# Another order of TensorE's work in each step of an attention: values of the preceding tile ahead of the second pair of scores, maxima behind it

## The chip, the cores and the metric

One core of a Trainium2 chip runs the whole program. The metric is the device time of one execution in microseconds, the median of several runs. One execution was also taken with the hardware profiler; its trace gives every row below.

## What is computed

The program is one block of a model on 8 batches of 256 channels and 1024 tokens: an attention with a position bias and a residual, a second attention with relative embeddings and a residual, and a routed feed-forward layer. The change is in the second attention only:

```
proj = jnp.einsum('bld,de->ble', x, W) + b            # x is (8, 1024, 256), normalised
q, k, v = jnp.split(proj.reshape(batch, length, 8, 96).transpose(0, 2, 1, 3), 3, axis=3)
qk = jnp.einsum('bhqd,bhkd->bhqk', q, k)
qe = jnp.einsum('bhqd,qkd->bhqk', q, embeddings)      # rotated sinusoids of q - k
weights = softmax((qk + qe) / sqrt(32), axis=-1)
output = jnp.einsum('bhqk,bhkd->bhqd', weights, v)
```

## The kernel before

The program runs its stages one after another: tables, the first token phase (projections), the first attention (names end in `_af`), the second token phase, the second attention (names end in `_kf`), and the feed-forward tail. Every engine has its own queue, worked off in the written order, and waits on semaphores.

The second attention works **keys first**: scores stand with keys on the partitions and queries along the free axis. A *unit* `u` is one batch, one group of four heads and 512 queries; there are 32 units. A unit has eight *steps*, one for each tile of 128 keys; step `n` counts through all units (256 steps), and `n % 8` is its place in the unit. In a step TensorE does, for the tile `n`:

- `scores(4n)`, the first pair: for heads 0 and 1 one product over 128 rows each (L1118), then one over 64 rows each (L1123) that adds the low halves and the row of maxima. The banks for scores are three, in a ring, so the score of head `s` waits until the exponential of `s - 3` has read its bank. `scores(4n + 2)` is the second pair, heads 2 and 3.
- `maxima(n)`: four products over 64 rows (L996) that form scores for the unit after next or the next one, only for their row maxima. VectorE reduces them (L1004, two in a step, in two banks used in turn). In step 6 a transpose of all row maxima of the next unit (L989) stands in front of them; VectorE copies it to `max_row` (L1006), and SyncE moves it with four small transfers (L981) into the row of `lows` that the next unit's scores read. The first scores of a unit wait for these transfers (semaphore `m_in`).
- `weigh(n - 1)`, the values of the preceding tile (L1143): four fp32 products of 32 columns each, side by side, added up over the unit in one bank, `out_ps`. They wait until all four exponentials of tile `n - 1` are there, and the first of a unit waits until the last unit's `out_ps` was copied (semaphore `taken`).
- `denominators`, the sums of the unit before, in step 1 (L1155): twelve fp32 products of the shape of L1143 over the last two tiles of exponentials and the sum of the other six, which GpSimd adds up (L1229). They go into one of the two banks of the maxima; VectorE copies them (L1248) and takes reciprocals in four pieces, one in each of steps 2 to 5 (L1242).

ScalarE takes the exponential of each head (L1199) into a ring of four tiles; for head 0 from the fifth tile on it also waits for the ring (`weighed`, and `acc_ok` or `max_full`). It copies the finished `out_ps` to `oS` (`take`, L1182) in the step that `TAKE` names, between heads 1 and 2. GpSimd multiplies and adds the residual behind its sums of step 5.

Of the kernel before, what the change touches and what calls it, by code (L numbers as in the profile page):

```python
# [10 lines left out]
def build(nc, x, gamma, wqkv, wout, w1q, b1cols, b1v, gatew, experts, relt, cw0, cb0, cw1, cb1, cw2, cb2,  # L11
# [30 lines left out]
    KTU = NT  # L42
# [14 lines left out]
    with ctx:  # L57
# [836 lines left out]
        def attention_keys_first():  # L894
            with ExitStack() as es:
# [31 lines left out]
                NU = NB * UB  # L927
# [43 lines left out]
                def queries(u):  # L971

                    return (u // NC) % G, (u % NC) * CH
# [10 lines left out]
                def max_product(pe, n, u, m, max_ps=max_ps):  # L984

                    slot, first = queries(u)
                    if m == MH:
                        pe.wait_ge(max_read, n)
                        nc.tensor.transpose(max_ps[n % len(max_ps)][0:HG * TT, 0:P], row_min[:], idf[:]).then_inc(max_full, 1)  # L989
                        return  # L990
                    if n >= len(max_ps):
                        pe.wait_ge(max_read, n + 1 - len(max_ps))
                    j, t = divmod(m, TT)
                    for c in range(NC):
                        half = slice(2 * D * c, 2 * D * (c + 1))
                        last = nc.tensor.matmul(max_ps[n % len(max_ps)][:, c * CH:(c + 1) * CH],  # L996
                                                stacks[half, slot, QHH, j, first + t * P:first + (t + 1) * P],
                                                stacks[half, slot, KHL, j, c * CH:(c + 1) * CH], start=True, stop=True)
                    last.then_inc(max_full, 1)
# [7 lines left out]
                                                ALU.mult).then_inc(max_read, 1)  # L1007

                AHEAD_ = KTU + 2
                DEN, REC, TAKE, FIN = 1, 2, 1, 5  # L1010
                first_jobs = [(0, m) for m in range(MJ)] + [(1, m) for m in range(2 * (AHEAD_ - KTU))]
                step_jobs = []
                for n in range(NU * KTU):
# [54 lines left out]
                with nc.Fori(0, B // NB) as i_:  # L1068
                    with nc.Block() as block:
# [37 lines left out]
                        @block.tensor  # L1107
                        def _(pe):
                            def scores(s):

                                u, (kt, j) = s // SU, divmod(s % SU, HG)
                                slot, first = queries(u)
                                if s % SU == 0 and u >= 1:
                                    pe.wait_ge(m_in[u % 2], 16 * HG * ((u + 1) // 2))
                                for i in range(2):
                                    if s + i >= 3:
                                        pe.wait_ge(exps, s + i - 2)
                                    nc.tensor.matmul(score_ps[(s + i) % 3], stacks[:, slot, KHL, j + i, kt * P:(kt + 1) * P],  # L1118
                                                     stacks[:, slot, QHH, j + i, first:first + CH], start=True, stop=False,
                                                     skip_group_check=True)  # L1120
                                for i in range(2):
                                    half = slice(2 * D * i, 2 * D * (i + 1))
                                    nc.tensor.matmul(score_ps[(s + i) % 3], lows[half, slot, KH1, j // 2, kt * P:(kt + 1) * P],  # L1123
                                                     lows[half, slot, QL, j // 2, first:first + CH], start=False, stop=True,
                                                     skip_group_check=True).then_inc(full, 1)

                            def maxima(n):
                                for u, m in step_jobs[n]:
                                    if m == 0 and u % NC == 0:
                                        q = u // NC  # L1130
                                        pe.wait_ge(stk[q % 2], LOADS * ((q + 1) // 2))
                                    max_product(pe, job_at[(u, m)], u, m)

                            def weigh(n):
                                u, kt = divmod(n, KTU)
                                g, bb = (u // NC) % G, u // UB
                                if kt == 0 and u % UB == 0 and bb >= 1:
                                    pe.wait_ge(v_in[bb % 2], 16 * ((bb + 1) // 2))
                                if kt == 0 and u >= 1:
                                    pe.wait_ge(taken, u)  # L1140
                                pe.wait_ge(exps, HG * (n + 1))
                                for j in range(HG):
                                    last = nc.tensor.matmul(out_ps[j * D:(j + 1) * D, :],  # L1143
                                                            V[:, bb % 2, kt, (g * HG + j) * D:(g * HG + j + 1) * D],
                                                            prob[:, n % PR, j, :], start=(kt == 0), stop=(kt == KTU - 1),
                                                            skip_group_check=True)
                                last.then_inc(weighed, 1)

                            def denominators(n, u):
                                pe.wait_ge(max_read, n - 1)  # L1150
                                pe.wait_ge(acc_ok, ADDS * (u + 1))
                                parts = [prob[:, (KTU * u + kt) % PR] for kt in range(ADDS + 1, KTU)] + [acc[:, u % 2]]
                                for i, part_ in enumerate(parts):
                                    for j in range(HG):
                                        last = nc.tensor.matmul(max_ps[n % 2][j * D:(j + 1) * D, 0:CH], den_w[:], part_[:, j, :],  # L1155
                                                                start=(i == 0), stop=(i == len(parts) - 1),
                                                                skip_group_check=True)
                                last.then_inc(max_full, 1)

                            for n in range(NU * KTU + DEN + 1):  # L1160
                                if n < NU * KTU:
                                    scores(HG * n)
                                summed = n >= KTU and n % KTU == DEN
                                if summed:
                                    denominators(job_at[(n // KTU - 1, "den")], n // KTU - 1)
                                elif n < NU * KTU:
                                    maxima(n)
                                if n < NU * KTU:
                                    scores(HG * n + 2)
                                    if summed:  # L1170
                                        maxima(n)
                                if 1 <= n <= NU * KTU:
                                    weigh(n - 1)

                        @block.scalar
                        def _(act):
# [26 lines left out]
                        def _(pool):  # L1203
                            def finish(u):

                                bb, g = u // UB, (u // NC) % G
                                _, first = queries(u)
                                pool.wait_ge(taken, u + 1)
                                pool.wait_ge(recd, PIECES * (u + 1))
                                if u >= 1:  # L1210
                                    pool.wait_ge(fin, u)
                                nc.gpsimd.tensor_tensor(oN[:], oS[:, u % 2, :], rec[:, u % 2, :], ALU.mult).then_inc(scaled, 1)
                                pool.wait_ge(x_in[bb % 2], 16 * (bb // 2 + 1))
                                pool.wait_ge(scaled, u + 1)
                                r = res_[:, bb % 2, g, first:first + CH]
                                nc.gpsimd.tensor_tensor(r, r, oN[:], ALU.add).then_inc(fin, 1)
# [266 lines left out]
        for kind, attention in enumerate((attention_first, attention_keys_first)):  # L1483
            stages = attention()
            early = next(stages)
            tables = setup(early) if kind == 0 else None
            token_phase(kind, early.rooms, early, tables)
            next(stages, None)
            if kind == 0:
                turned.close()  # L1490
# [493 lines left out]
```

## Time and profile before

| | before |
|---|---|
| median of 3 runs | 2847.14 us (2841.78 to 2848.37) |
| the profiled execution's own time | 2855.66 us |
| its span, first to last instruction | 2853.8 us |
| second attention, stretch 1509 to 2462 us of the span | 953 us |
| TensorE busy in it | 937.25 us |
| VectorE, ScalarE, GpSimd busy in it | 714.06, 571.87, 802.02 us |
| granted TensorE clock in it | 1.00 (2.4 GHz) |
| share of the 16 DMA engines in it | 0.24 |

A row of the timeline has the start in us from the span's start, the time from the first to the last instruction of the row, the engine (PE is TensorE's products, PEld its weight loads, DVE VectorE, ACT ScalarE, POOL GpSimd, SPq SyncE's queue), the line, what it writes and reads, the count, and in brackets how long the engine sat idle before it and what ended that. Products are pipelined: one of 512 columns is shown with some 0.39 us and the next one starts 0.21 us after it, so a wait between two products of one row shows as a longer row and not as idle time. What counts is from start to start.

### The profile page before, as it was taken

Reading aid. Unit: us, or ns where it says so; the run is one execution under the profiler, and the core shown is the slowest. Engines: PE = TensorE matmul, PEld = TensorE weight load, DVE = VectorE, ACT = ScalarE, POOL = GpSimd, SP = SyncE. Lnnn points to the kernel's source line nnn. Section 1 sums busy time; section 2 is a strip of 40 time slices with the busy share of each in tenths; the row PEclk is TensorE's granted clock in tenths of the full one; section 3 lists DMA queues with packets and bytes.
Section 4 is the critical chain, followed back from the end, with each engine's and each line's share of the span. In section 5 each row is a group of like instructions: output and inputs, shape, how many; then the busy total and the mean of one; then the engine's idle time right before and its main releaser. Section 6 shows DMA issues by size and latency. Waiting matters only on the chain. (4 is left out here: it accounts for less than half of the span.)

```text
span 2853.8 us, 47289 instructions
## 1 busy us (share of the span) xinstructions
PE 2481.0 (87%) x18516; PEld 817.5 (29%) x18516; DVE 1991.5 (70%) x3075; ACT 1402.8 (49%) x2548; POOL 1967.8 (69%) x763
## 2 busy tenths in 40 slices
PE   7899999999999999968988999999999999651255
PEld 2564222222222222235552222222222222240144
DVE  4475787787787787647886777877778777277134
ACT  3345555555555555523335565665656656440012
POOL 3114788888888888844446888888888888630763
PEclk9999999999999999989999999999999999775568
DMA  4994222322222322039764321223212230350337
GB/s 80 238 237 137 49 50 49 76 67 49 53 49 55 80 57 53 9 134 308 231 216 116 74 64 49 64 71 90 64 49 64 71 75 16 102 180 9 96 121 248
DMA packets 236267, 278.16 MB, mean 97 GB/s; under 512 B 65392, under 2 KB 171376, under 8 KB 232842
## 3 DMA queue, kind: packets, MB, share of 16 engines
q1 hardware_dynamic: 225548, 249.89, 32.3%
q0 software_dynamic: 6144, 16.85, 1.9%
q10 hardware_dynamic: 4352, 8.39, 0.8%
q8 instruction: 147, 2.41, 0.4%
q14 instruction: 76, 0.62, 0.1%
HBM read 165.17 MB, written 110.67 MB: 97 GB/s over the span
## 5 line engine op out<-in xcount | busy, mean ns | idle before, releaser
L854 POOL TENSOR_TENSOR room_af<-room_af 128x2048 f32<-128x2048 f32 x160 | 725.6, 4535 | 163.6 <-ACT room_af L826 149.8
L1229 POOL TENSOR_TENSOR bias<-bias 128x2048 f32<-128x2048 f32 x160 | 724.3, 4527 | 153.3 <-ACT bias L1199 134.1
L826 ACT ACTIVATE room_af<-PS 128x512 f32<-128x512 f32 x1024 | 555.9, 594 | 396.3 <-PE PS L748 396.3
L1199 ACT ACTIVATE bias<-PS 128x512 f32<-128x512 f32 x1024 | 555.9, 594 | 376.2 <-PE PS L1123 373.8
L635 DVE CUSTOM_DVE_ANT_0 PS<-PS,bias 128x1024 f32<-128x1024 f32 x512 | 620.1, 1241 | 160.6 <-PE PS L623 142.6
L1004 DVE TENSOR_REDUCE row_min_kf<-PS 128x1 f32<-128x1024 f32 x512 | 601.9, 1220 | 107.2 <-PE PS L996 98.6
L1118 PE MATMUL PS<-stacks_kf 128*128 128x512 f16 x1024 | 339.2, 387 | 15.3 <-PEq L90 8.5
L741 PE MATMUL PS<-QS_af,KS_af 128*128 128x512 f16 x1024 | 334.5, 387 | 14.3 <-PEq L90 4.5
L774 PE MATMUL PS<-room_af,V_af 128*32 128x512 f32 x2048 | 272.7, 605 | 1.2 <-ACT room_af L826 1.2
L1143 PE MATMUL PS<-bias,V_kf 128*32 128x512 f32 x2048 | 272.8, 605 | 0.2 <-ACT bias L1199 0.2
L748 PE MATMUL PS<-turned_bias,eyes 64*32 64x512 f16 x4096 | 210.6, 388 | 0.0
L1123 PE MATMUL PS<-lows_kf 64*128 64x512 f16 x1024 | 199.9, 387 | 0.0
L1118 PEld LDWEIGHTS PS<-stacks_kf 128*128 128x128 f16 x1024 | 72.2, 96 | 385.5 <-ACT bias L1199 253.2
L996 PE MATMUL PS<-stacks_kf 64*128 64x512 f16 x1024 | 165.6, 380 | 12.9 <-DMA stacks_kf<-query_key_halves 6.3
L623 PE MATMUL PS<-KM_af,QM_af 32*128 32x512 f16 x1024 | 128.5, 386 | 43.1 <-DVE row_min_af L635 31.3
L741 PEld LDWEIGHTS PS<-QS_af,KS_af 128*128 128x128 f16 x1024 | 70.9, 97 | 311.6 <-ACT room_af L826 234.9
L1784 POOL DMA_INDIRECT G_t<-token_rows,idxT_t x64 | 66.0, 1032 | 110.8 <-DVE valT_t L1899 91.6
L1699 PE MATMUL PS<-bias,gh_t 128*128 128x256 f16 x256 | 60.9, 337 | 91.4 <-DVE gl_t L1908 49.6
L1755 ACT CAST gh_t<-PS 128x256 f16<-128x256 f32 x64 | 23.5, 373 | 233.4 <-PE PS L1685 149.1
L413 POOL TENSOR_TENSOR room_af<-room_af 128x1024 f16<-128x1024 f32 x16 | 34.0, 2127 | 136.2 <-ACT room_af L370 136.2
L1248 DVE COPY bias<-PS 128x512 f32<-128x512 f32 x32 | 22.1, 692 | 142.8 <-PE PS L1155 142.8
L873 DVE RECIPROCAL room_af<-room_af 128x128 f32<-128x128 f32 x128 | 120.7, 947 | 1.1
(184 smaller groups left out, 3070.4 us busy)
## 6 DMA issues: line engine op xcount, KB each, us to landing
query_key_halves<-bias SPq DMA_DIRECT2D x32, 768.0 KB, 4.0
query_key_halves<-room_af SPq DMA_DIRECT2D x32, 512.0 KB
stacks_kf<-query_key_halves SPq DMA_DIRECT2D x64, 256.0 KB, 7.2
KS_af<-query_key_halves SPq DMA_DIRECT2D x48, 256.0 KB, 4.8
QS_af<-query_key_halves SPq DMA_DIRECT2D x48, 256.0 KB, 7.0
lows_kf<-query_key_halves SPq DMA_DIRECT2D x96, 128.0 KB
token_rows<-rows_t SPq DMA_DIRECT2D x16, 514.0 KB, 4.2
FT_t<-token_rows SPq DMA_DIRECT2D x16, 514.0 KB
```

The lines of the kernel that those rows point to most:

```text
L635: nc.vector.tensor_tensor_reduce(out=max_ps[n % len(max_ps)], in0=max_ps[n % len(max_ps)], in1=bias_h[:, g * HG + j, z:z + N], scale=-1.0, ...
L741: nc.tensor.matmul(score_ps[s % 3], KS[:, g, j, kt * P:(kt + 1) * P], QS_[:, g, j, first:first + CH], start=True, stop=False, skip_group_c ...
L748: last = nc.tensor.matmul(score_ps[(HG * n + 2 * pair + i) % 3][c * W:(c + 1) * W, :], eyes[half, :], turned_bias[half, 2 * g + pair, z:z ...
L774: last = nc.tensor.matmul(out_ps[j * D:(j + 1) * D, :], V[:, q % 2, kt, j * D:(j + 1) * D], prob[:, n % PR, j, :], start=(kt == 0), stop=( ...
L826: nc.scalar.activation(prob[:, n % PR, head, :], score_ps[s % 3], ACT.Exp).then_inc(exps, 1)
L854: nc.gpsimd.tensor_tensor(acc[:, u % 2], so_far, prob[:, n % PR], ALU.add).then_inc(acc_ok, 1)
L1004: nc.vector.tensor_reduce(row_min[:, m:m + 1], max_ps[n % len(max_ps)], AX.X, ALU.min).then_inc(max_read, 1)
L1118: nc.tensor.matmul(score_ps[(s + i) % 3], stacks[:, slot, KHL, j + i, kt * P:(kt + 1) * P], stacks[:, slot, QHH, j + i, first:first + CH], ...
L1123: nc.tensor.matmul(score_ps[(s + i) % 3], lows[half, slot, KH1, j // 2, kt * P:(kt + 1) * P], lows[half, slot, QL, j // 2, first:first + C ...
L1143: last = nc.tensor.matmul(out_ps[j * D:(j + 1) * D, :], V[:, bb % 2, kt, (g * HG + j) * D:(g * HG + j + 1) * D], prob[:, n % PR, j, :], st ...
L1199: nc.scalar.activation(prob[:, n % PR, j, :], score_ps[s % 3], ACT.Exp, scale=-1.0 / (W1S * W1S)).then_inc(exps, 1)
L1229: nc.gpsimd.tensor_tensor(acc[:, u % 2], so_far, prob[:, n % PR], ALU.add).then_inc(acc_ok, 1)
```

## The change

Two things are changed in the second attention. TensorE's order in a step was first pair, maxima, second pair, values of the preceding tile, and in step 1 of a unit first pair, sums, second pair, maxima, values. It is now the same in every step: first pair, values of the preceding tile, sums where there are any, second pair, maxima. And `TAKE` is 0 and not 1: ScalarE copies the finished values in step 0 of the next unit.

```diff
-                DEN, REC, TAKE, FIN = 1, 2, 1, 5
+                DEN, REC, TAKE, FIN = 1, 2, 0, 5
...
                             for n in range(NU * KTU + DEN + 1):
                                 if n < NU * KTU:
                                     scores(HG * n)
-                                summed = n >= KTU and n % KTU == DEN
-                                if summed:
+                                if 1 <= n <= NU * KTU:
+                                    weigh(n - 1)
+                                if n >= KTU and n % KTU == DEN:
                                     denominators(job_at[(n // KTU - 1, "den")], n // KTU - 1)
-                                elif n < NU * KTU:
-                                    maxima(n)
                                 if n < NU * KTU:
                                     scores(HG * n + 2)
-                                    if summed:
-                                        maxima(n)
-                                if 1 <= n <= NU * KTU:
-                                    weigh(n - 1)
+                                    maxima(n)
```

TensorE's queue of before, from the first pair of a step 1 to the first pair of step 2 (L1118 and L1123 are a pair of scores, L996 maxima, L1143 values, L1155 sums):

```order
L1118 MATMUL PS<-stacks_kf 128x512 x2
L1123 MATMUL PS<-lows_kf 128x512 x2
L1155 MATMUL PS<-bias,den_w_kf 32x512 x12
L1118 MATMUL PS<-stacks_kf 128x512 x2
L1123 MATMUL PS<-lows_kf 128x512 x2
L996 MATMUL PS<-stacks_kf 128x512 x4
L1143 MATMUL PS<-bias,V_kf 32x512 x4
L1118 MATMUL PS<-stacks_kf 128x512 x2
```

The same place in the changed kernel, on to the values in step 2:

```order
L1118 MATMUL PS<-stacks_kf 128x512 x2
L1123 MATMUL PS<-lows_kf 128x512 x2
L1143 MATMUL PS<-bias,V_kf 32x512 x4
L1155 MATMUL PS<-bias,den_w_kf 32x512 x12
L1118 MATMUL PS<-stacks_kf 128x512 x2
L1123 MATMUL PS<-lows_kf 128x512 x2
L996 MATMUL PS<-stacks_kf 128x512 x4
L1118 MATMUL PS<-stacks_kf 128x512 x2
L1123 MATMUL PS<-lows_kf 128x512 x2
L1143 MATMUL PS<-bias,V_kf 32x512 x4
```

The values moved up in front of the sums, and the maxima now stand last. The second place is step 6, where the transpose of the maxima (L989) stands; TensorE's queue of before, from the step's first pair:

```order
L1118 MATMUL PS<-stacks_kf 128x512 x2
L1123 MATMUL PS<-lows_kf 128x512 x2
L989 MATMUL PS<-idf,row_min_kf 16x128
L996 MATMUL PS<-stacks_kf 128x512 x4
L1118 MATMUL PS<-stacks_kf 128x512 x2
```

In the changed kernel, from the second pair of that step to the values in step 7:

```order
L1123 MATMUL PS<-lows_kf 128x512 x2
L989 MATMUL PS<-idf,row_min_kf 16x128
L996 MATMUL PS<-stacks_kf 128x512 x4
L1118 MATMUL PS<-stacks_kf 128x512 x2
L1123 MATMUL PS<-lows_kf 128x512 x2
L1143 MATMUL PS<-bias,V_kf 32x512 x4
```

The transpose moved behind the second pair, by values and one pair of scores nearer to the next unit. ScalarE's queue around its copy (L1182) in the kernel before; the waits are in brackets:

```order
L1199 ACTIVATE bias<-PS 128x512 [waits full_kf,acc_ok_kf,weighed_kf]
L1199 ACTIVATE bias<-PS 128x512 [waits full_kf]
L1182 COPY oS_kf<-PS 128x512 [waits scaled_kf,weighed_kf]
L1199 ACTIVATE bias<-PS 128x512 [waits full_kf] x2
L1199 ACTIVATE bias<-PS 128x512 [waits full_kf,max_full_kf,weighed_kf]
```

In the changed kernel that copy (now L1178, and the exponentials L1195) stands four exponentials earlier. The exponential of head 0 is the one with three waits; that of heads 1 to 3 has one.

## Rows read from the trace of the kernel before

**Rows 1.** Timeline of an ordinary step, 1819.7 to 1824.3 us; columns as above.

```profile
1819.71 0.60 PE L1118 MATMUL PS<-stacks_kf 128*128 128x512 f16 x2
...
1820.24 0.39 PE L1123 MATMUL PS<-lows_kf 64*128 64x512 f16 x2
...
1820.75 1.09 ACT L1199 ACTIVATE bias<-PS 128x512 f32<-128x512 f32 x2 [0.85 <-PE PS L1123]
...
1821.00 0.79 PE L1118 MATMUL PS<-stacks_kf 128*128 128x512 f16 x2
1821.40 0.10 PEld L1118 LDWEIGHTS PS<-stacks_kf 128*128 128x128 f16 x1 [0.31 <-ACT bias L1199]
...
1821.72 0.39 PE L1123 MATMUL PS<-lows_kf 64*128 64x512 f16 x2
...
1822.04 1.06 PE L1143 MATMUL PS<-bias,V_kf 128*32 128x512 f32 x8
1822.15 1.08 ACT L1199 ACTIVATE bias<-PS 128x512 f32<-128x512 f32 x2 [0.31 <-PE PS L1123]
...
1823.04 0.61 PE L1118 MATMUL PS<-stacks_kf 128*128 128x512 f16 x2
1823.16 0.94 DVE L1242 RECIPROCAL bias<-bias 128x128 f32<-128x128 f32 x1
...
1824.23 2.36 DVE L1004 TENSOR_REDUCE row_min_kf<-PS 128x1 f32<-128x1024 f32 x2
```

**Rows 2.** Timeline of TensorE and ScalarE in the attention's third step, still without ring waits.

```profile
1519.24 0.60 PE L1118 MATMUL PS<-stacks_kf 128*128 128x512 f16 x2
1519.78 0.39 PE L1123 MATMUL PS<-lows_kf 64*128 64x512 f16 x2
...
1522.49 0.60 PE L1118 MATMUL PS<-stacks_kf 128*128 128x512 f16 x2
...
1520.20 1.08 ACT L1199 ACTIVATE bias<-PS 128x512 f32<-128x512 f32 x2 [0.77 <-PE PS L1123]
```

**Rows 3.** Timeline of steps 1 and 2 of a unit, 1807 to 1817 us.

```profile
1807.02 0.60 PE L1118 MATMUL PS<-stacks_kf 128*128 128x512 f16 x2
...
1807.88 2.78 PE L1155 MATMUL PS<-bias,den_w_kf 128*32 128x512 f32 x24
...
1810.60 0.60 PE L1118 MATMUL PS<-stacks_kf 128*128 128x512 f16 x2
...
1812.72 23.20 POOL L1229 TENSOR_TENSOR bias<-bias 128x2048 f32<-128x2048 f32 x5 [3.84 <-ACT bias L1199]
...
1814.19 0.39 PE L996 MATMUL PS<-stacks_kf 64*128 64x512 f16 x2 [0.17 <-DVE row_min_kf L1004]
...
1816.37 0.60 PE L1118 MATMUL PS<-stacks_kf 128*128 128x512 f16 x2
```

**Rows 4.** Timeline at the transposes of two units: TensorE, and SyncE's move.

```profile
1797.53 0.28 PE L989 MATMUL PS<-idf,row_min_kf 128*16 128x128 f32 x1
...
1827.23 0.28 PE L989 MATMUL PS<-idf,row_min_kf 128*16 128x128 f32 x1
...
1827.85 2.44 SPq L981 DMA_DIRECT2D lows_kf<-max_row_kf  x4
...
1828.20 0.61 PE L1118 MATMUL PS<-stacks_kf 128*128 128x512 f16 x2
```

**Rows 5.** Timeline of the first attention's last move of maxima and its copy of values.

```profile
1189.24 2.44 SPq L607 DMA_DIRECT2D QS_af<-max_row_af  x4
...
1192.73 0.11 PEld L741 LDWEIGHTS PS<-QS_af,KS_af 128*128 128x128 f16 x2 [1.02 <-DMA QS_af<-max_row_af]
...
1194.80 0.59 ACT L808 COPY room_af<-PS 128x512 f32<-128x512 f32 x1
```

**Rows 6.** Timeline at the second attention's end: the last exponentials and the last values.

```profile
2455.37 1.08 ACT L1199 ACTIVATE bias<-PS 128x512 f32<-128x512 f32 x2 [0.31 <-PE PS L1123]
...
2456.50 1.07 PE L1143 MATMUL PS<-bias,V_kf 128*32 128x512 f32 x8 [0.17 <-ACT bias L1199]
```

## Prediction

> **What bounds the kernel now.** I read the stage table first: in the second attention TensorE is busy 937.25 of 953 us at a clock of 1.00, the other engines far less. But its rows stretch over waits inside them, so I went to the timeline and took distances from start to start. An ordinary step takes 3.33 us (1819.71 to 1823.04) [rows 1]. Its pieces: a pair of scores 0.53 to its L1123; from there over the maxima to the next pair 0.76; from an L1123 to the values 0.32; the values 1.00. Without a wait the step would be 0.53 + 0.76 + 0.53 + 0.32 + 1.00 = 3.14 us. The missing 0.19 is in the second pair: that row is 0.79 long where a free one is 0.60, and its second weight load at 1821.40 is released by ScalarE [rows 1]. It is the score of head 3, which needs the bank that head 0's exponential reads.
>
> So the step is set by a loop: a pair's L1123, the exponential, and behind the maxima the second product of the next pair. With the pieces: from L1123 to the exponential's start 0.51 (1820.24 to 1820.75), to the product that it frees 0.65 (1820.75 to 1821.40), together 1.16; TensorE's own way there is 0.76 + 0.21 = 0.97 (0.21 is 0.53 less the 0.32 from the second product to L1123). 1.16 - 0.97 = 0.19 [rows 1]. Behind the values there is no such wait, since 1.00 us of other work covers it.
>
> A unit takes 29.70 us (1797.53 to 1827.23) [rows 4]. Steps 1 and 2 take 9.35 together (1807.02 to 1816.37): the sums add 2.72 (1807.88 to 1810.60), and in step 2 the maxima follow the last ones so closely that TensorE waits for VectorE (1814.19) [rows 3].
>
> **The change, part by part.** *The order of ordinary steps.* Before, the cycle is first pair, maxima, second pair, values; after, it is first pair, values, second pair, maxima. As kinds of work both are the same ring, pair, maxima, pair, values, with the same changes of shape. What differs is which pair has the maxima behind it: it was the first, it will be the second. The two pairs' exponentials don't start equally soon: 0.51 us after L1123 for heads 0 and 1, 0.43 for heads 2 and 3 (1821.72 to 1822.15) [rows 1]. Head 0's instruction has three waits, head 2's one (the queue in the section on the change). That the waits and not the place cause the 0.08 is seen in the third step of all, where head 0 waits for no ring yet: there the first pair's exponential starts 0.42 after L1123, in front of the same maxima, and the step takes 3.25 us (1519.24 to 1522.49) [rows 2]. The Trainium skill says in "Perfetto Trace Analysis", "Identifying Dependency Chains", that an instruction which waits on several engines may get extra semaphore instructions in front of it, which would be this kind of cost; no run here shows them apart.
>
> After the change the loop runs over the second pair: 0.43 + 0.65 = 1.08, against the same 0.97. The wait falls from 0.19 to 0.11, the step to 3.25 us. The later start of head 0's exponential costs nothing: behind the first pair come the values, 1.00 + 0.32 + 0.21 = 1.53 us to the product that needs it, against 1.16.
>
> *Does the moved `weigh` wait?* It needs the exponential of head 3 of the preceding tile. At the end of the attention that wait shows: the values start 1.13 us after the pair's exponentials (2455.37 to 2456.50) [rows 6]. So they could start 0.43 + 1.13 = 1.56 after the second pair's L1123. In the new order they stand 1.08 + 0.32 (second product to L1123) + 0.32 = 1.72 after it: 0.16 us to spare, cost nothing.
>
> *Steps 1 and 2.* The sums now follow the values in the same shape. Alone they take 2.72 for three times four products, where the values take 1.00 for four; so each further four costs (2.72 - 1.00) / 2 = 0.86, and behind the values the sums add 3 x 0.86 = 2.58, say 2.57. Maxima of steps 1 and 2 are now a whole step apart, and the wait for VectorE goes; the bank that VectorE has to copy out is needed 0.2 us later than the first one, as before. Steps 1 and 2 take 3.25 + 2.57 + 3.25 = 9.07, against 9.35.
>
> *Step 6 and 7.* The transpose puts 1827.23 to 1828.20, 0.97, plus 0.32 in front of the next pair in place of 0.76: 0.53 more, and its cover takes the exponential wait of the pair behind it [rows 1, 4]. Step 6 takes 3.25 + 0.53 = 3.78, step 7 3.14.
>
> *The unit.* 9.07 + 3 x 3.25 (steps 3 to 5) + 3.78 + 3.14 + 3.25 (step 0) = 28.99 us, against 29.70: 0.71 less. Some 0.58 of it is the exponential's start, 0.13 the sums.
>
> *The move of the maxima.* The transpose moves back by values and a pair, the next unit's first scores don't. From the transpose to them there will be 0.97 + 0.53 + 0.32 + 1.00 + 0.53 + 0.76 = 4.11 us; SyncE issues the first of four transfers 0.62 after it (1827.85) [rows 4], which leaves 3.49. The first attention shows this wait once in plain sight: weight load 3.49 us after the first issue (1189.24 to 1192.73), with the same four transfers of 1 KB and the same 2.44 us for issuing them [rows 5]. And the first 0.11 of a delay would only take the place of the wait for the exponential. So it fits, with nothing to spare; cost 0, at most what the rival below gives.
>
> *TAKE.* In step 0 the values of the last tile start 0.53 + 0.11 + 0.32 = 0.96 after the first pair and their row is 1.06 long; ScalarE has done heads 0 and 1 at 0.64 + 0.51 + 1.09 = 2.24. The copy, 0.59 like that of the first attention [rows 5], ends at 2.83, and head 2 is ready at 1.96 + 0.53 + 0.43 = 2.92. It lies in idle time. With `TAKE` still 1, `weigh` of step 1 would wait for a copy behind it.
>
> *GpSimd.* Its five additions start 2.12 us after the second pair of step 1 (1810.60 to 1812.72) and take 23.20 [rows 3]. That pair comes 0.64 + 0.32 + 1.00 + 2.57 = 4.53 after the step's start, so they end at 29.85; the ring lets head 0 of the next step 1 go then, and it would want to at 28.99 + 0.64 + 0.51 = 30.14. Free by 0.29 us. VectorE has 2.36 + 0.94 = 3.30 of row time in steps 2 to 5 [rows 1]; rows next to each other overlap a little (the reductions are followed within 2.27 where 2.36 is their length), so I take 3.21, under 3.25. Were it 3.30, those four steps would cost 0.05 each, 6 us in all.
>
> *The sum.* 30 full units x 0.71 = 21.3. The first unit has half its steps at 3.25 already: 0.3. In the last unit the end is set by the chain of GpSimd's additions, which start 4.53 + 2.12 = 6.65 after step 1 begins and not 5.70 [rows 3]: 0.95 back; its first scores come sooner after the last transpose, with no maxima between, and wait some 0.3. In all 21.3 + 0.3 - 0.95 - 0.3 = 20.4 us. From the profiled execution's 2855.7 that makes 2835.3; it lies 8.5 above the median of the runs, so against the median 2847.1 the forecast is **2826.7 us**.
>
> **The rivals.**
> *A: the step stays at 3.33.* If the 0.08 belonged to the place behind which a pair stands, the new order would move it along and the ring would be the same as before. Left is the saving at the sums and around the transpose, 30 x 0.14 = 4.2, less the last unit's 1.25: 2844 us. Rows 2 speak against it. Chance 0.09.
> *B: the maxima land late.* Nothing is to spare beyond 0.11. If they took till 3.9 after the first issue, the unit start would wait 0.3, 31 times: gain 11, 2836 us. Only one row shows the landing, in the other attention. The Trainium skill ("DMA: Bandwidth & Descriptors", "Anatomy of one DMA") gives about 2 us of fixed cost for one transfer; behind the last of four issues, some 1.87 after the first, that would be 3.87, and an estimate by it is 0.27 late, 8 us of the gain lost. The row says 1.62 for the same. Chance of a loss of over 5 us: 0.12; from 4.31 on it would be no gain.
> *C: the values wait, and it gets slower.* The loop second pair, exponentials, values, second pair is now 1.56 + 1.00 + 0.53 = 3.09 without its first waits and has 0.16 us free. If the exponentials were seen later, by a longer start on ScalarE behind `weigh`'s own waits, every step would wait on it: from 0.16 + 0.09 = 0.25 late the kernel is no faster, at 0.35 it is 25 us slower, 2872. What speaks for it: the order asks for the newest exponentials sooner than the old one did. Against: rows 6 measure just this distance. Chance 0.07.
> *D: something of both small kinds* (VectorE at 3.30, GpSimd 0.3 late): gain 10 to 15, 2834. Counted with the forecast.
>
> **How the numbers follow.** Forecast (gain of 10 to 24) 0.72; A 0.09; B 0.12; C 0.07. About 0.3%, 8.5 us, is what a measurement tells from no change. B is faster in two thirds of its cases: faster 0.72 + 0.08 = 0.80, same 0.09 + 0.03 = 0.12, slower 0.08. The runs of before lie 6.6 us apart, so a median may be off by 3. The range reaches from a gain of 24 and 3 to A's edge: 2820 to 2844.
>
> **What would show it.** In the timeline: ordinary steps of 3.25, with L1123 of the second pair 1.08 before the second product of the next first pair, where the wait now is; values behind the first pair with no idle time from ScalarE; steps 1 and 2 of 9.07; no weight load released by VectorE in step 2; a unit of 28.99; the unit's first weight load 3.5 after the first issue, released by DMA or by nothing. Wrong would be: a unit start that waits over 0.2 us, steps of 3.33, or values released by ScalarE in ordinary steps.

## The result and the profile after

The changed kernel takes 2825.05 us (median of 4 runs, 2824.42 to 2828.49), the kernel before 2846.84 (4 runs): a ratio of 0.9929, 95% interval 0.9912 to 0.9946. It is faster by 21.8 us; the forecast was 2826.7. Nearly all of it lies in the second attention, as the table of stages shows; each length is from the first L1118 of the attention to the end of its last addition on GpSimd, in one profiled execution (that addition's row starts at 2469.83 and 2451.93 and is 1.26 long).

| | before | after |
|---|---|---|
| first L1118 | 1508.42 | 1510.09 |
| end of the last addition of the residual | 2471.09 | 2453.19 |
| second attention | 962.67 | 943.10 |
| from there to the end of the span | 382.7 | 369.4 |
| span | 2853.8 | 2822.6 |
| unit, transpose to transpose | 29.70 | 29.03 |

The spans differ by 31.2 us, more than the medians. 13 us of that is in the feed-forward tail, which neither order touches: in the eight runs below it took 367.7 to 373.0 us, so the profiled execution of before was long there by some 10 us. That fits the 8.5 by which it lay above the median of its kernel. The attention itself gained 19.6.

The timeline of the changed kernel in an ordinary step (line numbers behind `denominators` are four lower than before: L1195 is L1199, L1178 is L1182, L1225 is L1229):

```profile
1816.18 0.60 PE L1118 MATMUL PS<-stacks_kf 128*128 128x512 f16 x2
...
1816.72 0.39 PE L1123 MATMUL PS<-lows_kf 64*128 64x512 f16 x2
...
1817.14 1.08 ACT L1195 ACTIVATE bias<-PS 128x512 f32<-128x512 f32 x2 [0.69 <-PE PS L1123]
...
1817.47 0.71 PE L1118 MATMUL PS<-stacks_kf 128*128 128x512 f16 x2
1817.79 0.10 PEld L1118 LDWEIGHTS PS<-stacks_kf 128*128 128x128 f16 x1 [0.23 <-ACT bias L1195]
...
1818.12 0.39 PE L1123 MATMUL PS<-lows_kf 64*128 64x512 f16 x2
...
1818.44 0.16 PEld L1143 LDWEIGHTS PS<-bias,V_kf 128*32 128x32 f32 x8 [0.23 <-ACT bias L1195]
1818.44 1.07 PE L1143 MATMUL PS<-bias,V_kf 128*32 128x512 f32 x8
1818.62 1.08 ACT L1195 ACTIVATE bias<-PS 128x512 f32<-128x512 f32 x2 [0.40 <-PE PS L1123]
...
1820.73 0.71 PE L1118 MATMUL PS<-stacks_kf 128*128 128x512 f16 x2
```

The step is 3.26 us (1817.47 to 1820.73), against 3.33 [rows 1]. The row of 0.60 is now the second pair and the stretched one, 0.71, the first: the loop has changed pairs. The second pair's exponential starts 0.42 behind L1123 (1816.72 to 1817.14), and 0.65 later the weight load that it frees follows (1817.79): 1.07, where the old loop had 1.16. The first pair's exponential still starts 0.50 behind its L1123 (1818.12 to 1818.62), now in front of the values.

The weight load of the values names ScalarE as its releaser, as three in four do in the view of waits from 1500 to 2440 us:

```profile
PEld PS L1143 <- ACT bias L1195: 44.7, 192, 1.5
```

That is no wait of the values: 0.23 also stands in front of each of the 64 that are put down to "issue" (14.5 us in all), and 44.7 less the one long wait of 1.5 is 0.23 for each of the other 191. The preceding tile's last exponentials end at 1818.22 (1817.14 and 1.08), and [rows 6] show that values can start 0.05 after such an end; so 0.17 is to spare, forecast 0.16.

Steps 1 and 2 of a unit in the changed kernel, timeline:

```profile
1801.89 0.71 PE L1118 MATMUL PS<-stacks_kf 128*128 128x512 f16 x2
...
1802.85 1.06 PE L1143 MATMUL PS<-bias,V_kf 128*32 128x512 f32 x8
...
1803.73 2.76 PE L1155 MATMUL PS<-bias,den_w_kf 128*32 128x512 f32 x24
...
1806.42 0.60 PE L1118 MATMUL PS<-stacks_kf 128*128 128x512 f16 x2
...
1808.55 13.88 POOL L1225 TENSOR_TENSOR bias<-bias 128x2048 f32<-128x2048 f32 x3 [3.16 <-ACT bias L1195]
...
1810.97 0.71 PE L1118 MATMUL PS<-stacks_kf 128*128 128x512 f16 x2
```

They take 9.08 us (1801.89 to 1810.97) against 9.35 [rows 3]. Values and sums together take 3.57 (1802.85 to 1806.42), and the product that waited for VectorE in step 2 has no counterpart. The end of one unit and the start of the next, timeline:

```profile
1794.52 0.28 PE L989 MATMUL PS<-idf,row_min_kf 128*16 128x128 f32 x1
...
1823.55 0.28 PE L989 MATMUL PS<-idf,row_min_kf 128*16 128x128 f32 x1
...
1824.17 2.44 SPq L981 DMA_DIRECT2D lows_kf<-max_row_kf  x4
...
1827.67 0.10 PEld L1118 LDWEIGHTS PS<-stacks_kf 128*128 128x128 f16 x1 [0.43 <-DMA lows_kf<-max_row_kf]
...
1829.79 0.59 ACT L1178 COPY oS_kf<-PS 128x512 f32<-128x512 f32 x1
...
1830.59 1.08 ACT L1195 ACTIVATE bias<-PS 128x512 f32<-128x512 f32 x2 [0.21 <-PE PS L1123]
```

The unit's first weight load comes 3.50 us after the first of the four transfers is issued (1824.17 to 1827.67) and is released by DMA; in the first attention it was 3.49 [rows 5]. The copy lies in ScalarE's idle time: the next exponential still waits for TensorE, 0.21. In the same view of waits this release stands with its total; almost all of it is the weight load's ordinary gap of 0.42. So at nearly every unit start TensorE's own work takes as long as the transfers, and the rows there don't show how much sooner they may have landed. TensorE itself waited twice, most of it at the last unit:

```profile
PEld PS L1118 <- DMA lows_kf<-max_row_kf: 14.3, 31, 1.2
...
PE PS L1118 <- DMA lows_kf<-max_row_kf: 1.1, 2, 0.9
```

Timeline of these two unit starts:

```profile
1853.20 2.73 SPq L981 DMA_DIRECT2D lows_kf<-max_row_kf  x4
...
1857.00 0.61 PE L1118 MATMUL PS<-stacks_kf 128*128 128x512 f16 x2 [0.23 <-DMA lows_kf<-max_row_kf]
...
2408.60 0.60 PE L1118 MATMUL PS<-stacks_kf 128*128 128x512 f16 x2 [0.86 <-DMA lows_kf<-max_row_kf]
```

At the first of them SyncE took 2.73 us to issue the four and not 2.44, the scores came 3.80 after the first issue, and the unit took 29.23 us. The other 30 starts lie at 3.49 to 3.53.

### The profile page after: what moved, and what is told of

Read it like the earlier page. It is cut to its first block and busy times, and to the rows that moved or that the text cites. A ratio compares the mean times of both kernels' runs of the same rounds, so it can differ in the third digit from the quotient of the medians.

```text
span 2822.6 us, 47289 instructions
## 1 busy us (share of the span) xinstructions
PE 2467.3 (87%) x18516; PEld 822.8 (29%) x18516; DVE 1989.9 (70%) x3075; ACT 1403.2 (50%) x2548; POOL 1967.6 (70%) x763
## 5 line engine op out<-in xcount | busy, mean ns | idle before, releaser
L1225 POOL TENSOR_TENSOR bias<-bias 128x2048 f32<-128x2048 f32 x160 | 724.6, 4529 | 133.2 <-ACT bias L1195 114.4
L1195 ACT ACTIVATE bias<-PS 128x512 f32<-128x512 f32 x1024 | 555.7, 594 | 356.0 <-PE PS L1123 354.6
L1118 PE MATMUL PS<-stacks_kf 128*128 128x512 f16 x1024 | 334.9, 387 | 12.6 <-PEq L90 8.5
L1143 PE MATMUL PS<-bias,V_kf 128*32 128x512 f32 x2048 | 272.7, 605 | 1.2 <-ACT bias L1195 1.2
L1123 PE MATMUL PS<-lows_kf 64*128 64x512 f16 x1024 | 199.9, 387 | 0.0
L1118 PEld LDWEIGHTS PS<-stacks_kf 128*128 128x128 f16 x1024 | 75.6, 96 | 376.0 <-ACT bias L1195 248.0
L996 PE MATMUL PS<-stacks_kf 64*128 64x512 f16 x1024 | 160.4, 379 | 7.1 <-DMA stacks_kf<-query_key_halves 5.5
L1238 DVE RECIPROCAL bias<-bias 128x128 f32<-128x128 f32 x128 | 119.8, 940 | 0.1
L748 PEld LDWEIGHTS PS<-turned_bias,eyes 64*32 64x32 f16 x4096 | 57.4, 89 | 186.0 <-issue 186.0
```

Source lines behind the costliest of these rows:

```text
L748: last = nc.tensor.matmul(score_ps[(HG * n + 2 * pair + i) % 3][c * W:(c + 1) * W, :], eyes[half, :], turned_bias[half, 2 * g + pair, z:z ...
L1143: last = nc.tensor.matmul(out_ps[j * D:(j + 1) * D, :], V[:, bb % 2, kt, (g * HG + j) * D:(g * HG + j + 1) * D], prob[:, n % PR, j, :], st ...
L1195: nc.scalar.activation(prob[:, n % PR, j, :], score_ps[s % 3], ACT.Exp, scale=-1.0 / (W1S * W1S)).then_inc(exps, 1)
L1225: nc.gpsimd.tensor_tensor(acc[:, u % 2], so_far, prob[:, n % PR], ALU.add).then_inc(acc_ok, 1)
```

## The experiments

Theory **W**: the order gains because an exponential with three waits starts 0.08 us later than one with one wait, and the order moves the loop from the pair that has them to the pair that doesn't. Rival **P**: the 0.08 belongs to a pair's place in the step. (The rival is A of the prediction.) The first four runs put the same two waits in different places. They ran on one chip; before took 2845.37 there.

### Ring waits moved, old order

```diff
-                                if n >= PR and j == 0:
-
-                                    u, kt = divmod(n - PR, KTU)
-                                    act.wait_ge(weighed, n - PR + 1)
+                                t = n + 1 if j == 3 else n
+                                if PR <= t < NU * KTU and j == (0 if t % KTU == 1 else 3):
+                                    u, kt = divmod(t - PR, KTU)
+                                    act.wait_ge(weighed, t - PR + 1)
```

> Old order, TAKE 1; ScalarE's two ring waits are taken off head 0 and put on head 3 of the preceding tile (in step 1 they stay on head 0). Theory W (the waits on head 0's instruction make its exponential start 0.08 us later, and the old order has that pair in the loop): the start falls from 0.51 to 0.43 us behind L1123, five to six steps of a unit go from 3.33 to 3.25 us, unit 29.7 to 29.3, 12 us off the kernel. Rival P (the 0.08 belongs to the place of the pair in the step): start stays 0.51, time as before within 3 us.

Measured: 2834.58 us, ratio 0.9958 (0.9943 to 0.9974), 10.8 us faster than before; attention 949.91 us, 12.8 less; unit 29.30. Its timeline:

```profile
1821.04 0.60 PE L1118 MATMUL PS<-stacks_kf 128*128 128x512 f16 x2
1821.57 0.39 PE L1123 MATMUL PS<-lows_kf 64*128 64x512 f16 x2
...
1821.99 1.08 ACT L1199 ACTIVATE bias<-PS 128x512 f32<-128x512 f32 x2 [0.77 <-PE PS L1123]
...
1824.29 0.60 PE L1118 MATMUL PS<-stacks_kf 128*128 128x512 f16 x2
```

The first pair's exponential starts 0.42 and not 0.51 behind L1123, and the step is 3.25, with TensorE's queue untouched. P falls: place and order are those of before. The unit is shorter by 0.41 (29.70 to 29.30), five steps of 0.08. Steps 1 and 2 still take 9.34 together (9.35 before), so this edit gets nothing of what the new order gains there.

### The same waits on head 2 too, old order and new

```diff
-                                if n >= PR and j == 0:
+                                if n >= PR and j % 2 == 0:
```

In the old order:

> Old order; head 2 gets the same ring waits as head 0, besides head 0's own. Theory W: head 2's exponential starts 0.51 and not 0.43 behind its L1123, but behind it stand the values, 1.00 us of cover, so the time is that of before within 2 us. Rival P: nothing changes either; this run is the control for the same edit in the new order.

Measured: 2847.62 us, ratio 1.0004 (0.9995 to 1.0013). Timeline:

```profile
1822.93 0.39 PE L1123 MATMUL PS<-lows_kf 64*128 64x512 f16 x2
...
1823.43 1.08 ACT L1199 ACTIVATE bias<-PS 128x512 f32<-128x512 f32 x2 [0.40 <-PE PS L1123]
```

Head 2 now starts 0.50 behind L1123 where it was 0.43 [rows 1], and the time doesn't move, since the values cover it. In the new order:

> New order; head 2 gets the same ring waits as head 0. They are met long before, so they cost only their handling. Theory W: head 2 starts 0.51 behind L1123, the loop is as slow as in the old order, ordinary steps 3.33, unit about 29.6, 15 to 18 us slower than the changed kernel, that is 2 to 5 us faster than before. Rival P: no change against the changed kernel.

Measured: 2844.66 us, ratio 1.0000 to before (0.9990 to 1.0009), 19.6 above the changed kernel's median and 18.8 above the next run, which was taken together with this one; attention 960.43, 17.3 above the changed kernel's; unit 29.60. The two added waits take back all that the change gave but 2 us of the attention. They are met whenever head 2 comes to them, since head 0's exponential has just waited for the same, so what they cost is their handling. Timeline, with the 0.50 and the wait that follows from it:

```profile
1815.96 0.79 PE L1118 MATMUL PS<-stacks_kf 128*128 128x512 f16 x2
...
1818.54 0.39 PE L1123 MATMUL PS<-lows_kf 64*128 64x512 f16 x2
...
1819.04 1.08 ACT L1195 ACTIVATE bias<-PS 128x512 f32<-128x512 f32 x2 [0.77 <-PE PS L1123]
...
1819.29 0.79 PE L1118 MATMUL PS<-stacks_kf 128*128 128x512 f16 x2
```

The step is 3.33 again and the pair's row 0.79 long, as in [rows 1]. One edit, no cost in the one order and nearly the whole gain in the other: what counts is whether the pair is in the loop. What one further wait costs, and not two, was not tried.

### Ring waits moved, new order

The diff is that of the first run, in the changed kernel.

> New order, TAKE 0, the ring waits moved as in the first of these runs. Theory W: head 0's exponential starts 0.08 sooner, but it is not in the loop any more, so the time is that of the changed kernel within 2 us, unit 29.03. If the two effects were independent (the order gains by something else than the waits), it would be 10 to 12 us faster than the changed kernel.

Measured: 2825.89 us, ratio 0.9937 (0.9921 to 0.9953); attention 943.09, unit 29.03, to a hundredth those of the changed kernel. The gains of the order and of moved waits don't add, since both take the same 0.08 out of the loop.

### TAKE alone, and the order alone

The other four ran together; before took 2846.57 there. First `TAKE = 0` in the old order:

```diff
-                DEN, REC, TAKE, FIN = 1, 2, 1, 5
+                DEN, REC, TAKE, FIN = 1, 2, 0, 5
```

> Old order, TAKE 0. The values of a unit's last tile then stand behind the second pair of step 0, and ScalarE waits for them in step 0 with the exponentials of heads 2 and 3 behind the copy. Theory: those start about 1.7 us later (0.32 + 1.19 + 0.59 behind L1123 and not 0.43), the second product of step 1 waits for head 2's some 1 us, unit 29.7 to 30.8, 32 us slower than before. Rival (ScalarE has room everywhere, busy 60% of the stage): no change.

Measured: 2879.54 us, ratio 1.0110 (1.0094 to 1.0126), 33.0 slower; attention 994.07, unit 30.77. In its timeline the copy stands behind the late values, and the second product of step 1 waits for the exponential behind it:

```profile
1820.19 0.39 PE L1118 MATMUL PS<-stacks_kf 128*128 128x512 f16 x1
1820.32 0.59 ACT L1182 COPY oS_kf<-PS 128x512 f32<-128x512 f32 x1 [1.34 <-PE PS L1143]
1820.80 1.09 ACT L1199 ACTIVATE bias<-PS 128x512 f32<-128x512 f32 x2
...
1821.46 0.39 PE L1118 MATMUL PS<-stacks_kf 128*128 128x512 f16 x1 [0.89 <-ACT bias L1199]
```

The changed kernel with `TAKE` put back to 1 (the same line the other way):

> New order, TAKE 1. The first values of a unit then stand ahead of the copy of the last unit's values: they wait till 0.64 + 0.51 + 1.08 + 0.59 + 0.06 = 2.9 us into step 1 and not 0.96. Theory: 1.9 us more in each step 1, unit 30.96, 60 us slower than the changed kernel and 38 to 42 slower than before. Rival (the sums behind the values cover part of it): under half of that.

Measured: 2890.04 us, ratio 1.0147 (1.0131 to 1.0162), 43.5 slower than before, where 38 to 42 was expected; attention 1004.64, unit 30.84. Timeline:

```profile
1825.63 0.71 PE L1118 MATMUL PS<-stacks_kf 128*128 128x512 f16 x2
...
1827.75 0.59 ACT L1178 COPY oS_kf<-PS 128x512 f32<-128x512 f32 x1
1828.40 0.16 PEld L1143 LDWEIGHTS PS<-bias,V_kf 128*32 128x32 f32 x8 [2.03 <-ACT oS_kf L1178]
1828.40 1.06 PE L1143 MATMUL PS<-bias,V_kf 128*32 128x512 f32 x8 [1.73 <-ACT oS_kf L1178]
```

The values wait for the copy till 2.77 into the step, where the changed kernel has them at 0.96 (1801.89 to 1802.85 above). Three of the 30 units took 32.53 to 32.63 us, 1.7 to 1.8 longer than the others; without these 5 us the run would lie inside the expectation. There TensorE's clock fell behind that wait. In one of them, the timeline and then three stretches of one microsecond each (TensorE's busy time stands behind the length; the last three numbers are granted clock, DMA share and GB/s):

```profile
1672.47 1.14 PE L1143 MATMUL PS<-bias,V_kf 128*32 128x512 f32 x8 [1.83 <-ACT oS_kf L1178]
```

```profile
1672.00:1673.00 1.00, 0.53 (x8) 0.23 (x12) 0.00 (x0) 0.41 (x1) 0.87 (x1) 1.00 0.00 0
...
1674.00:1675.00 1.00, 1.00 (x8) 0.22 (x4) 0.00 (x0) 0.00 (x0) 0.00 (x0) 0.50 0.00 0
...
1677.00:1678.00 1.00, 1.00 (x10) 0.11 (x2) 0.13 (x1) 0.00 (x0) 0.00 (x0) 1.00 0.00 0
```

TensorE sat idle 1.83 us, worked again for less than a microsecond at a granted clock of 1.00, and then had 0.50, the lower level of 1.2 GHz, over most of the sums. The other units waited 1.73 to 1.81 at the same place and kept the clock; why just three lost it is not shown. Each half of the change loses 1% and more; together they gain.

### The old order in step 1 only

```diff
-                                if 1 <= n <= NU * KTU:
+                                summed = n >= KTU and n % KTU == DEN
+                                if 1 <= n <= NU * KTU and not summed:
                                     weigh(n - 1)
-                                if n >= KTU and n % KTU == DEN:
+                                if summed:
                                     denominators(job_at[(n // KTU - 1, "den")], n // KTU - 1)
                                 if n < NU * KTU:
                                     scores(HG * n + 2)
                                     maxima(n)
+                                if 1 <= n <= NU * KTU and summed:
+                                    weigh(n - 1)
```

> Changed kernel, but step 1 has the old order: first pair, sums, second pair, maxima, values; the other seven steps the new one. Theory: the sums change shape once more, 0.15 us, and the maxima of steps 1 and 2 stand apart by the values of two tiles, so no wait for VectorE; unit 29.2 to 29.3, 5 to 7 us slower than the changed kernel. Rival (the 0.58 of the unit's gain comes from step 1 and 2 and not from the ordinary steps): 15 us or more slower.

Measured: 2833.58 us, ratio 0.9951 (0.9936 to 0.9966), 8.5 above the changed kernel; attention 950.07, 7.0 longer; unit 29.28, 0.25 longer. So step 1's order is a third of the gain and the other steps two thirds. Timeline:

```profile
1831.10 0.16 PEld L1155 LDWEIGHTS PS<-bias,den_w_kf 128*32 128x32 f32 x8 [0.44 <-DVE row_min_kf L1004]
1831.10 2.78 PE L1155 MATMUL PS<-bias,den_w_kf 128*32 128x512 f32 x24
1833.81 0.11 PEld L1118 LDWEIGHTS PS<-stacks_kf 128*128 128x128 f16 x2 [0.84 <-issue]
...
1835.10 1.07 PE L1143 MATMUL PS<-bias,V_kf 128*32 128x512 f32 x8
...
1836.10 0.11 PEld L1118 LDWEIGHTS PS<-stacks_kf 128*128 128x128 f16 x2 [0.84 <-ACT bias L1198]
```

The sums alone take 2.71 and the values alone 1.00, 3.71 in place of 3.57: 0.14. The expectation was wrong in saying that nothing waits for VectorE. The sums, which go into a bank of the maxima, do: their weight load has 0.44 in front of it where the ordinary gap is 0.23, which is 0.21 more, 30 times in the view of waits. In step 2 the first pair stands behind values and not behind maxima, so the exponential's wait of 0.11 is missing there. 0.14 + 0.21 - 0.11 = 0.24, and the unit is 0.25 longer.

### A fifth transfer in front of the four

```diff
+    spare = nc.dram_tensor("spare_maxima", [64, 512], F16).ap()
...
+                    sp.dma_start(spare[u].rearrange("(t n) -> t n", n=P), max_row[0:TT, u % 2, :]).then_inc(m_in[u % 2], 16)
                     for j in range(HG):
```

The three places that wait for the unit's four transfers now wait for five.

> Changed kernel with one more transfer of 1 KB, into an unused array in HBM, issued in front of the four that move the maxima; the unit waits for it too. Theory: the four land 0.61 us later, at 4.11 behind the first issue, where the unit's first scores stand at 3.49; 0.11 of it takes the place of the exponential's wait, so 0.5 us per unit, 31 times: 15 to 16 us slower than the changed kernel. Rival (the landing has more room than the one row said, or the move is not on the path): 0 to 5 us slower.

Measured: 2837.70 us, ratio 0.9967 (0.9955 to 0.9979), 12.7 above the changed kernel; attention 950.08, 7.0 longer; unit 29.23, 0.20 longer. Timeline (L980 and L983 are the fifth and the four):

```profile
1826.34 0.27 SPq L980 DMA_DIRECT2D spare_maxima<-max_row_kf  x1
1826.66 2.44 SPq L983 DMA_DIRECT2D lows_kf<-max_row_kf  x4
...
1830.16 0.11 PEld L1120 LDWEIGHTS PS<-stacks_kf 128*128 128x128 f16 x2 [0.76 <-DMA lows_kf<-max_row_kf]
1830.17 0.60 PE L1120 MATMUL PS<-stacks_kf 128*128 128x512 f16 x2 [0.27 <-DMA lows_kf<-max_row_kf]
```

The expectation was wrong in one number: the added transfer moved the four by 0.32 us (1826.34 to 1826.66) and not by 0.61. From the first of the four to the weight load it is 3.50 again. 0.32 less the 0.11 that replaces the exponential's wait gives 0.21; the unit is 0.20 longer. The rival falls all the same: at every unit start TensorE itself now waits, 31 times and 8.6 us in all. The medians lie further apart than the profile's 7 us. The profiled execution is the fastest of six (2831.14 to 2840.45), so the unit's 0.20 holds for it alone; whether the slower ones wait longer at each start is not shown.

## Why the prediction was right

**The loop and the exponential's start** carried the forecast, 0.58 of the unit's 0.71, and this is what the runs show: 1.16 to 1.07, step 3.33 to 3.26; the waits moved away give the same step in the old order, the waits added take it back in the new one, 0.57 of the unit (29.03 to 29.60). Rival A is refuted by both. Its price was right too: it put a new order with steps of 3.33 at 2844 us, and the run with the waits on head 2 took 2844.66.

**The values don't wait** in ordinary steps: their weight load follows the pair in 0.32 as forecast (1818.12 to 1818.44). The prediction had named values released by ScalarE as a sign of being wrong. The name does stand there, with no more than the ordinary gap of 0.23, so the sign was badly put: it should have asked for a longer gap. Rival C did not come; how far the 0.16 of room reaches was not tried.

**Steps 1 and 2**: 9.08 measured, 9.07 forecast. Values and sums 3.57 measured and forecast. VectorE held up neither step, and GpSimd's additions start 6.66 into step 1 (1801.89 to 1808.55), 6.65 forecast.

**The move of the maxima**: 3.49 to 3.53 against 3.49 at 30 of 31 unit starts. That nothing is left to spare was right too: 0.32 more and each unit pays 0.20. But one row of the first attention was thin ground, and part of this was luck. One start came at 3.80, a wait of 0.23 and so over the 0.2 that the prediction had called wrong. In other runs single starts came at 3.84 and 4.33, though the four were issued in the ordinary 2.42. Had that been common, it would have been rival B. B's price has a slip: with a gain of 20.4 over 31 starts nothing is left from 4.26 on, and not 4.31. Its estimate by the Trainium skill ("DMA: Bandwidth & Descriptors", "Anatomy of one DMA"), 3.87, isn't borne out here; the last of four issues starts some 1.87 after the first, and 1.63 later the load goes. That section describes transfers issued by GpSimd, and these are issued by SyncE.

**TAKE**: in idle time, as forecast, and needed. Its absence costs more than the whole gain.

**The sum**: unit 29.03 against 28.99, so 0.67 and not 0.71 less, some hundredths in each of several steps (ordinary ones 3.25 to 3.26, step 7 3.16 and not 3.14); over 30 units 1.2 us. The attention gained 19.6, forecast 20.4. In the last unit's start TensorE waited 0.86 for the maxima, part of it in place of the exponential's wait: the second product came some 1.46 behind L1123 (1.25 to the first, and 0.21), where the exponential alone would have let it go at 1.08. That is 0.38 late; I had put 0.3. The remaining 2 us to the medians' 21.8 are within the interval.

## What to carry to other kernels

When a ring of buffers sets the pace, write the loop out from start to start and ask which instruction of it has more waits than its sisters: put the instruction with more waits where other work covers it, or hang its waits on an earlier instruction. A reorder of the same pieces can gain mostly by that, and it needs its partners moved too: here either half by itself lost over 1%. Before moving a producer later, look for a place in the same trace where its transfer's landing is the wait. One such row tells what is to spare in the usual case, and several would tell how often it comes later. When a sign names a releaser, say how long the gap must be: the name stands in the profile also where nothing waits.

## What the runs showed of the hardware

Two further waits on a ScalarE instruction, met before it came to them, put off its start behind the third by 0.07 to 0.09 us (0.42 or 0.43 to 0.50 or 0.51), on head 0 and on head 2 alike. A transfer of 1 KB from four partitions took SyncE 0.27 us to issue when it went to HBM, and each of four into one partition's row some 0.6 (2.44 for four), from the same source. The two differ in the memory and in the layout that they write to, and no run tells these apart.

Where TensorE waited for these four, its weight load came 3.49 us after the first issue in the first attention and at the last unit of the changed kernel, and 3.48 to 3.53 at 30 starts of the run with a fifth transfer. Where issuing them took 2.73 or 2.77 and not 2.42 to 2.44, it came at 3.79 to 3.84. Single starts came late without a longer issue: 3.84 in the run with the waits on head 2 in the new order, 4.33 in the one with the old order in step 1.

TensorE's granted clock, 1.00 in this attention, fell to 0.50 in three units of the run with the order alone, each time behind a wait of some 1.8 us in step 1 (1.73, 1.78 and 1.83), and was back at 1.00 some 5 us after that wait. The other units of that run waited 1.73 to 1.81 there and kept 1.00.
